# One head-blocked attention layer with a sign-weight branch: paired products and projections, split steps ahead of the joining maximum, a last output finished on VectorE

## What is computed

```python
xn = layernorm(x)
q = relu(xn @ Wq.T + bq); k = relu(keys @ Wk.T + bk); v = relu(values @ Wv.T + bv)
score = einsum('bhsd,bhtd->bhst', qh, kh) / sqrt(16.)
a = einsum('bhst,bhtd->bhsd', softmax(score), vh)
a = transpose(a, (0, 1, 3, 2)).reshape(q.shape)      # head-wise transposed
y = clip(xn @ sign(weights).T * scale + bias, -100, 100)
out = x + (a + xn) + y
```

## Time and profile before

| | |
|---|---|
| median of 3 runs | 2849.71 us (2847.73 to 2850.22) |
| the profiled execution | 2850.59 us, its span 2848.8 us |
| PE matmuls busy | 2770.7 us, 97% |
| ACT busy | 2450.2 us, 86% |
| DVE busy | 2337.4 us, 82% |
| POOL busy | 938.4 us, 33% |
| granted PE clock, mean | 0.983 |

### The profile page before, as it was taken

The page is one execution under the profiler, slowest core; times in us unless marked ns, Lnnn a source line. Parts: engine busy times, 40 slices in busy tenths (PEclk is TensorE's granted clock), DMA queues, the critical chain, the costliest instruction groups (busy, mean ns, idle before and its releaser), DMA issues.

```text
span 2848.8 us, 61155 instructions
## 1 busy us (share of the span) xinstructions
PE 2770.7 (97%) x17860; PEld 1149.8 (40%) x17860; DVE 2337.4 (82%) x4578; ACT 2450.2 (86%) x2949; POOL 938.4 (33%) x845
## 2 busy tenths in 40 slices
PE   8899999999999999999999999999999999999996
PEld 4434444443444434444443444434444443444331
DVE  6788888888888888888888888888888888888940
ACT  4688888888888888888888888888888888888996
POOL 4304334242343314333242343314333242343001
PEclk8699999999999999999999999999999999999998
DMA  7111121121221121121121221121121121211111
GB/s 142 60 40 55 65 70 36 56 70 55 65 70 52 40 70 55 65 66 33 62 69 55 65 66 49 47 70 55 65 64 35 62 68 56 65 62 37 48 55 38
DMA packets 78637, 167.74 MB, mean 59 GB/s; under 512 B 28548, under 2 KB 32647, under 8 KB 76327
## 3 DMA queue, kind: packets, MB, share of 16 engines
q1 hardware_dynamic: 78374, 164.19, 19.2%
HBM read 36.71 MB, written 17.83 MB: 19 GB/s over the span
## 4 chain that ended last, share of the span: by engine, by line
PE 79%; issue 10%; DVE 7%; ACT 2%; POOL 1%; DVEq 0%; DMA 0%; POOLq 0%; ACTq 0%
PE value_ps L611 30%; PE ring L633 28%; PE score_ps L597 13%; DVE mx L959 5%; ACT probs L806 2%; PE score_ps L677 1%; PE score_ps L662 1%; PE score_ps L679 1%; PE score_ps L666 1%; PE score_ps L664 1%; PE ring L720 1%; POOL fin L1097 1%; PE score_ps L715 0%; DVE excess L934 0%; PE ring L700 0%
## 5 line engine op out<-in xcount | busy, mean ns | idle before, releaser
L806 ACT ACTIVATE probs<-score_ps 128x1024 f32<-128x1024 f32 x2048 | 1992.3, 1024 | 236.1 <-PE score_ps L597 229.9
L959 DVE TENSOR_REDUCE mx<-ring 128x1 f32<-128x512 f32 x2952 | 1900.1, 684 | 248.8 <-PE ring L633 224.5
L633 PE MATMUL ring<-kstack,qstack 48*128 48x512 f32 x3444 | 1168.4, 467 | 16.7 <-DVE mx L959 3.1
L611 PE MATMUL value_ps<-probs,vones 128*32 128x512 f32 x8192 | 1092.3, 605 | 1.1 <-ACT taken L813 0.4
L633 PEld LDWEIGHTS ring<-kstack,qstack 48*128 48x128 f32 x3444 | 490.1, 184 | 1071.0 <-DVE mx L959 1034.3
L597 PE MATMUL score_ps<-qstack,kstack 51*128 51x512 f32 x4096 | 814.1, 416 | 13.8 <-ACT probs L806 4.5
L934 DVE CUSTOM_DVE_ANT_0 excess<-ring,excess 128x512 f32<-128x512 f32 x512 | 353.1, 690 | 136.7 <-PE ring L633 119.1
L1097 POOL TENSOR_TENSOR dense<-dense,affine 128x512 f32<-128x512 f32 x128 | 164.4, 1284 | 866.7 <-ACT dense L856 865.2
L597 PEld LDWEIGHTS score_ps<-qstack,kstack 51*128 51x128 f32 x4096 | 393.6, 186 | 132.1 <-ACT probs L806 70.5
L822 ACT ACTIVATE excess<-ring 128x512 f32<-128x512 f32 x492 | 294.0, 597 | 1.4 <-PE ring L633 1.2
L611 PEld LDWEIGHTS value_ps<-probs,vones 128*32 128x32 f32 x8192 | 161.5, 108 | 320.7 <-issue 289.1
(11 more groups left out here) (93 smaller groups left out, 1417.2 us busy)
## 6 DMA issues: line engine op xcount, KB each, us to landing
qstack<-parts SPq DMA_DIRECT2D x768, 64.0 KB, 2.5
fin<-taken SPq DMA_DIRECT2D x256, 128.0 KB, 2.9
xin<-x SPq DMA_DIRECT2D x16, 1024.0 KB, 5.1
base_cur<-base_new SPq DMA_DIRECT2D x16, 1024.0 KB, 5.3
fin<-recip SPq DMA_DIRECT2D x32, 512.0 KB
out<-fin SPq DMA_DIRECT2D x32, 512.0 KB, 2.6
qstack<-proj SPq DMA_DIRECT2D x256, 12.0 KB
kstack<-base_cur SPq DMA_DIRECT2D x16, 128.0 KB, 6.0
```

What stands on the lines that cost most here:

```text
L611: mm = pe.matmul(value_ps[h4 * 32:(h4 + 1) * 32, :], vones[:, 2 * tp + c, hh * HALF + side * PAIRS + 2 * g + j, :, :], probs[:, q % 2 * GR ...
L633: pe.matmul(ps[:, :], qstack[nh][rows, pair, st * P:(st + 1) * P], keys, start=True, stop=True).then_inc(s_mm, 1)
L806: nc.scalar.activation(probs[:, q % 2 * GROUP + u % GROUP, :], score_ps[src][:, :], ACT.Exp, scale=EXP_SCALE).then_inc(s_probs, 1)
L959: nc.vector.tensor_reduce(most, src[:, :], AX.X, ALU.max).then_inc(s_mx, 1)
```

## The change

It does four things. (1) Two dense products, or two projections, go into one score tile, one in each bank; ACT takes both with one instruction of 1024 columns. Half 0 has jobs in duos 2, 8 (dense pairs) and 11 (projection pair), half 1 in duos 1, 3 (turns) and 9 (projection pair). (2) Split steps 0 and 1 stand ahead of the join of duo 25, steps 2 to 4 ahead of the join of duo 27; ROWS_DUO is 27; all eight aggregates stand ahead of the join of duo 23. (3) POOL's `base` works in pairs. (4) The last half's output is finished on DVE in two halves of the columns (`finish_end`), without packing, DRAM and POOL, and SP writes each half when it is ready. The start part keeps its single jobs.

```diff
-        JOBS = [[("dense", k, None) for k in range(2 * NA)] + [("project", a, 1) for a in range(NA)],
-                [("turn", a, None) for a in range(NA)] + [("project", a, 0) for a in range(NA)]]
-        JOB_DUOS = [[2, 4, 6, 8, 11, 13], [1, 3, 7, 9]]
+        JOBS = [[("dense", (2 * a, 2 * a + 1), None) for a in range(NA)] + [("project", (0, 1), 1)],
+                [("turn", (a,), None) for a in range(NA)] + [("project", (0, 1), 0)]]
+        JOB_DUOS = [[2, 8, 11], [1, 3, 9]]
         LEAD = 32
-        ROWS_DUO = 26
+        ROWS_DUO = 27
         RECIP_UNIT = 14
+        JOINS = 6
+        SPLIT_STEPS = {TILES + JOINS: (0, 1), TILES + 8 + JOINS: (2, 3, 4)}
         AGGREGATE_DUO = 23
...
@@ SP, half_step @@
+                if last and not (now or att):
+
+                    result = out[NB - 1].rearrange("(f p j) c -> f p (j c)", f=2, p=P)[1]
+                    for a in range(NA):
+                        cols = slice(a * BANK, (a + 1) * BANK)
+                        sp.wait_ge(s_end, 3 * a + 3)
+                        sp.dma_start(result[:, cols], fin[:, 1, cols]).then_inc(s_out, 16)
+                    return
...
@@ PE, do_job @@
+                    pe.wait_ge(s_xs, nb * NA + last + 1)
+                    ps = tile(b, to, s_qr, 4, oc * 2 + last + 1, hh)
                     cols = slice(oc * P, (oc + 1) * P)
+                    for n, k in enumerate(ks):
+                        dst = ps[:, n * BANK:(n + 1) * BANK]
...
+                    mm.then_inc(s_q, len(ks))
...
+                    for n, k in enumerate(ks):
+                        for j in range(2):
+                            dst = ps[:, (2 * n + j) * H:(2 * n + j + 1) * H]
...
@@ ACT, take_job @@
-                    nc.scalar.activation(proj[:, k, :], score_ps[src][:, 0:BANK], ACT.Relu,
-                                         bias=bq_sb[:, oc:oc + 1]).then_inc(s_qr, 1)
+                    act.wait_ge(s_q, nb * 4 + oc * 2 + last + 1)
+                    nc.scalar.activation(proj[:, first:last + 1, :],
+                                         score_ps[src][:, 0:len(ks) * BANK].rearrange("p (n s) -> p n s", s=BANK),
+                                         ACT.Relu, bias=bq_sb[:, oc:oc + 1]).then_inc(s_qr, len(ks))
...
+                    wait(act, s_badd, nb * 4 + last - 1)
+                    act.wait_ge(s_f, nb * 4 + last + 1)
                     ps = value_ps if src is None else score_ps[src]
+                    nc.scalar.activation(dense[:, first % 2:last % 2 + 1, :],
+                                         ps[:, 0:len(ks) * BANK].rearrange("p (n s) -> p n s", s=BANK),
+                                         ACT.Copy).then_inc(s_dense, len(ks))
...
@@ DVE @@
+            def finish_end(a):
+
+                cols = slice(a * BANK, (a + 1) * BANK)
+                dve.wait_ge(s_gather[a], NB * 4 * 32)
+                nc.vector.reciprocal(fin[:, 1, cols], fin[:, 1, cols]).then_inc(s_end, 1)
+                dve.wait_ge(s_end, 3 * a + 1)
+                nc.vector.tensor_tensor(fin[:, 0, cols], fin[:, 0, cols], fin[:, 1, cols], ALU.mult).then_inc(s_end, 1)
+                dve.wait_ge(s_bcopy, NB * 16)
+                dve.wait_ge(s_end, 3 * a + 2)
+                nc.vector.tensor_tensor(fin[:, 1, cols].rearrange("p (q j) -> p q j", j=J),
+                                        base_cur[:, 1, cols].rearrange("p (q j) -> p q j", j=J),
+                                        fin[:, 0, cols].rearrange("p (j q) -> p q j", j=J), ALU.add).then_inc(s_end, 1)
...
                         for n in itertools.chain(*maxima_of(d)):
                             if prep and d in STATS_DUOS and n % 8 in STATS_AHEAD:
                                 statistics(b, *ROW_TILES[2 * STATS_DUOS.index(d) + STATS_AHEAD.index(n % 8)])
+                            if prep and d == AGGREGATE_DUO and n % 8 == JOINS - 1:
+                                dve.wait_ge(s_stats, (b + 2) * 8)
+                            for k in SPLIT_STEPS.get(n, ()):
+                                split_maxima(b, hh, k, b * 2 * REDS + made(hh, TILES - 1))
+                            if prep and d == AGGREGATE_DUO and n % 8 == JOINS:
+                                for a, j in ROW_TILES:
+                                    aggregate(a, j)
                             reduce_bank(b, hh, n, at)
-                            if n >= TILES and not is_difference(n) and reductions(n - TILES) <= 5:
-                                split_maxima(b, hh, reductions(n - TILES) - 1,
-                                             b * 2 * REDS + made(hh, TILES - 1))
-                    if last and d == RECIP_UNIT // 2:
+                    if last and (now or att) and d == RECIP_UNIT // 2:
                         reciprocals(*last)
-                    if prep and AGGREGATE_DUO <= d < AGGREGATE_DUO + 4:
-                        for a, j in ROW_TILES[2 * (d - AGGREGATE_DUO):2 * (d - AGGREGATE_DUO) + 2]:
-                            aggregate(a, j)
...
@@ POOL, base @@
-                scaled(0)
-                shifted(0)
-                for k in range(1, 4):
+                for k in range(0, 4, 2):
                     scaled(k)
-                    clipped(k - 1)
                     shifted(k)
-                    if k == 3:
-                        pool.wait_ge(s_aff, whole * 2 + 8)
-                    summed(k - 1)
-                clipped(3)
-                summed(3)
+                    scaled(k + 1)
+                    clipped(k)
+                    shifted(k + 1)
+                    pool.wait_ge(s_aff, whole * 2 + 2 * k + 4)
+                    summed(k)
+                    clipped(k + 1)
+                    summed(k + 1)
```

## The result

The changed kernel takes 2873.38 us (median of 4 runs, 2869.72 to 2875.63) against 2849.89 us (4 runs, 2847.73 to 2850.22) on the same chip: 1.0084 times as long, interval 1.0073 to 1.0096, or 23.5 us more. Forecast were 2876 us and a range of 2850 to 2888. So the sign and the size came out.

What follows compares the result with a forecast made beforehand. TensorE (PE) was taken to bound the kernel, nearly full. Terms of +22.3+6.9+7.2+1.4-11.7 = +26.1 us on the profiled 2850.6 gave 2876.7, 2876 us as the median; range 2850 to 2888.

Steps and rivals of the forecast that it cites:

- The turn: Row maxima's turn behind banks 6 and 7 of duo 27, waiting for split step 4: +0.72 us each, 31 times, +22.3 us.
- joins 27 to 29 about 6.0 us apart: Sign that the forecast is right: this spacing of DVE's joining maxima around the turn, in every half.
- the wait for mcols: Sign that the forecast is right: the turn's weight load on PE waits near 1 us for mcols.
- Rival B: PE's wait on DVE in the next octet takes up the turn's slip: -22.3 us, 2854; chance 0.10.
- Steps 0 and 1: First two split steps, in DVE's 0.36 us hole ahead of the join of duo 25: cost nothing.
- the free lateness: In the plain octet, a join may be late by about 0.13 us for nothing.
- Dense pairs: Two dense products with one wide ACT copy that delays the relu and bank 5: +0.23 us a pair, +6.9 us.
- Rival A: The wider copies hold nobody, as relu and exponential find enough slack: 2856; chance 0.15.
- Projection pairs: Wider copy delays the exponential, which holds the second scores' tile: +0.24 us a pair, 30 pairs, +7.2 us.
- Aggregates: All eight ahead of the join of duo 23, 0.64 us against 0.49 free: +0.1 us in 14 batches, +1.4 us.
- The end: Last half finished on DVE, with a 512-element reciprocal of 3.4 us: span ends at 2837.1, -11.7 us.
- Row transfers and GpSimd's base: Rows land with 1.3 us in hand; the second base pair ends later, but its transfers are wanted late: cost 0.

Runs made afterwards that it cites:

- run 5: Kernel before with the turn alone moved (ROWS_DUO = 27), split steps where they were: 2857.96 us, ratio 1.0032.
- Run 6: Changed kernel with ScalarE's copy of a dense pair cut to 512 of 1024 columns, second product left out of the output: 2864.30 us.
- Run 2: Kernel before with the moved split steps, aggregates and turn alone: 2873.45 us, ratio 1.0081.
- Run 4: Changed kernel with the turn one duo later (ROWS_DUO = 28): 2879.65 us, ratio 1.0107.
- run 1: Kernel before with the new end alone: 2837.05 us against 2850.01, ratio 0.9957.
- run 3: Kernel before with the products and projections in pairs alone: 2860.15 us, ratio 1.0039.
- run 9: Kernel before with the new end, and half 1's reciprocal moved ahead of the reduction of bank 3 of duo 7: 2832.48 us.
- run 8: Kernel before with the new end, products and projections in pairs, dense pair behind banks 1 and 2, its copy behind the relu: 2856.76 us.

## Why the prediction was right, and where it wasn't

The measure is the octets before and after, per batch of 171.3 us.

- **The turn, forecast +0.72 a half.** Measured for the whole move is +0.82 in half 1 and +0.85 in half 0. In half 1 the octet of duo 27 is 0.20 longer than one without a turn and that of duo 29 0.73, 0.93 together in place of the forecast 1.10; less the 0.38 of before that is +0.55. In half 0 the two are 0.51 and 0.74 longer, because of the slower cast, and it is +0.85. That the average of the two is near the forecast is luck. "The turn loads at -0.45+0.75 = 0.30" was nearly right: counted from where the join would have been, it loads at 0.21. What was wrong is "Everything behind the turn on PE (scores, bank 0, weighing, bank 1) is 1.10 us late, and by the cycle above that is the octet's cost": the join of duo 27 stands behind the same split steps and moves by 0.20 with them, and bank 0 loads 0.75 us behind that join because of the ring, here and in run 5, though the turn of run 5 is 0.27 us earlier and waits for no split step. So of the signs, "joins 27 to 29 about 6.0 us apart" did not come (5.64), and the wait for mcols is 0.58 us in half 1 and 0.87 in half 0, not near 1. I had read who waits for the turn, and not which bank the tile behind it takes. Rival B (no dearer than today) is excluded by the octets of 5.64.
- **Steps 0 and 1, forecast nothing: wrong.** They cost 0.28 us in half 1. "0.28 and 0.1 against 0.36 and 0.13" took the pitch of the second from a place in which other work follows. In the lines above step 0 to step 1 is 0.39 us and step 1 to the join 0.35, 0.74 for both; less the hole of 0.36 and the free lateness of 0.13 that leaves 0.25. So the 0.13 of free lateness fits to 0.03 us.
- **Dense pairs, forecast +0.23 each: size right, wait half right.** Measured 7.39 + 4.91 - 12.10 = +0.20. Rival A (octets of 7.0) falls. Run 6 shows both halves of the step, the 0.20 saved and the 0.43 lost to the copy (0.37). It doesn't separate bank 5 from the scores' tile, which I had put into the bounds alone and which waits longer (0.71).
- **Projection pairs, forecast +0.24 each: too high.** The pair's octet is 7.67 us (7.72 forecast) and the one behind it 5.06 (5.15), together 12.73 against 12.62 of the two single ones: +0.11 in half 0, and +0.07 in half 1, so 2.7 us in 15 batches and not 7.2. The wait for the exponential is there and longer than forecast (0.31 against 0.25), but only 0.15 us of it reaches the octet behind (5.06 against a plain 4.91). The part that failed is that the wait's "+0.25 us on PE" goes into the time in full; what takes up the rest was not tried. The third octet, 5.04, is the same in both kernels.
- **Aggregates, forecast +0.1 in half 0, and "GpSimd's root starts earlier, and nobody waits for it".** Run 2 against run 5, which differ in the split steps and aggregates alone: +0.54 us in half 0 and +0.47 in half 1, so +0.07 for the aggregates. But the sum hides three parts: octet 23 gets 0.10 longer, octet 25 gains 0.11 where in half 1 it loses 0.27, and octet 27 loses 0.55 where in half 1 it loses 0.20. Some 0.3 us of this last loss is the cast of step 3: in each kernel with the moved aggregates (the changed one, runs 2, 4 and 6) 14 of 32 of these casts take 0.46 to 0.49 us, and these 14 are the ones beside GpSimd's `xn`, which starts earlier behind the earlier aggregates; the other 18 have no GpSimd work beside them and take 0.2, as all do in the kernels without the move. That is 4 us of the change's loss which the forecast did not see. Why the cast takes longer is not shown, and no run parts the aggregates from the split steps.
- **The end, forecast -11.7 us: right** (-11.6 in the trace and in run 1). The reciprocal of 512 elements is 3.35 us (forecast 3.4). The Trainium skill's repeat count of 8 (VectorE: DVE Perf Modes, "First, the fixed hardware budget"), from which I had worked out an estimate of 4.3 us, is not borne out: the two lengths of the trace, 543 ns for 64 elements and 3354 ns for 512, give 6.3 ns an element and 0.14 us beside. The last addition is 1.03 and not 0.69 us; its operands are strided.
- **Row transfers and GpSimd's base, forecast nothing: right.** The list of waits has one wait for rows, 1.4 us in the start part, and none in a batch; no engine waits longer for GpSimd in a batch (the slower cast above is no wait). Run 4 shows the price when the rows come 2 us later.
- **The sum.** Turn and split steps forecast 22.3 and aggregates 1.4, measured 1.65 x 15 = 25; pairs forecast 14.1, measured 0.53 x 15 = 8; end -11.7 and -11.6. The first is 1 too low and the second 6 too high, so the forecast terms come to 21 and not to 26.1. That the medians differ by 23.5 and the profiled executions by 24.2 is luck in part: the first batch of the loop has 4 us from the fall of the clock, and the start part gives 2 back.

The rule of the Trainium skill that the forecast cites (VectorE: DVE Perf Modes, "The TRN2 errata"), that fixed costs are paid per instruction and large tiles spread them, holds for ScalarE's copy (1.03 us against 2 x 0.60) and not for the kernel: run 3 shows the loss.

## What to carry to other kernels

Before an operation is put into a rotating set of buffers, write down which buffer each of the next users takes with it and when that one comes free; the right gap was two tiles away from the wrong one, and worth 0.5 us of 0.74. Short dependent operations cost more when they stand together, so spread them among other work rather than collect them in the widest hole. Work that starts earlier can also fall beside an instruction that then takes longer: look at the durations of unchanged instructions too, and not only at waits. And a merged copy on an engine with idle time is still dear when something short is queued behind it or a double-buffered tile hangs on it.

## What the runs showed of the hardware

**Small dependent VectorE operations.** Before, each split step has a reduction behind it that doesn't need it; the timeline of the kernel before:

```profile
1208.85 0.28 DVE L968 TENSOR_REDUCE mneg<-mx 128x64 f32<-128x128 f32 x1
1209.04 0.68 DVE L959 TENSOR_REDUCE mx<-ring 128x1 f32<-128x512 f32 x1
1209.64 0.19 DVE L973 CAST mcols<-mneg 128x64 bf16<-128x64 f32 x1
1209.74 0.69 DVE L959 TENSOR_REDUCE mx<-ring 128x1 f32<-128x512 f32 x1
```

The reduction begins 0.19 us after step 0 and 0.10 after step 1, before either has ended. With the dependent step right behind, step 0 keeps the engine for 0.39 us (1226.73 to 1227.12). All five steps take 0.71 us of DVE when spread (0.19, 0.10, 0.13, 0.10 and 0.19) and 1.55 us in two groups (1226.73 to 1227.47 and 1231.77 to 1232.58). Of the 0.84 us between them 0.45 lie between dependent steps. The other 0.39 lie between the last step of a group and the join, which doesn't need it (0.35 and 0.33 from start to start); the profile names nothing that holds the join there. The Trainium skill (VectorE: DVE Perf Modes, "The DRAIN you can't avoid") says of a chain of copies that a semaphore after each costs nothing and that the next operation does not start until the pipe is empty, but also that one which is not held starts earlier; its section "Rules for kernel authors" advises to minimize the count of operations and not the semaphores. This trace agrees with the earlier start (0.10 us behind a step of 0.19). It disagrees with the advice for operations of 0.2 us: at the same count, the order doubles the time.

**The clock after a short idle.** In the profiled execution of the changed kernel TensorE's granted clock falls to half (1.2 of 2.4 GHz) behind the entry of the loop. The columns are busy us of PE, PEld, DVE, ACT and POOL, then the granted clock, DMA share and GB/s:

```profile
194.00:198.00 4.00, 2.68 (x19) 0.90 (x15) 3.66 (x7) 2.59 (x4) 0.00 (x0) 1.00 0.16 63
198.00:202.00 4.00, 3.87 (x21) 2.01 (x22) 1.69 (x4) 2.85 (x4) 0.00 (x0) 0.72 0.22 78
202.00:206.00 4.00, 4.00 (x18) 1.53 (x17) 2.39 (x4) 2.33 (x4) 0.00 (x0) 0.50 0.17 66
206.00:210.00 4.00, 4.00 (x18) 1.82 (x16) 1.40 (x4) 1.72 (x2) 0.00 (x0) 0.50 0.29 66
```

PE had been idle for 1.38 us just ahead, with no releaser in the profile. The kernel before has the same idle time (1.34 us) at the same place and stays at 1.00. All 14 profiled executions are idle there for 1.15 to 1.40 us, and in 3 the clock falls: in the changed kernel and run 9 for about 10 us, in run 6 for about 3. In the changed kernel it costs 4.3 us (octets of 8.59 and 9.52 where run 3 has 6.42 and 7.39). So an idle time of 1.3 us may or may not cost a further 4 us. In the start part the full clock comes back only at 120 to 122 us (run 1, the changed kernel) or at about 126 (the kernel before), not at 105 as the section on the time before has it, and the octet there is 7.5 to 7.8 or 9.6 to 10.1 us. Kernels with and without each part of the change are in both groups. Part of the spread of the runs is this: the 8 runs of the kernel before beside runs 1 to 4 go from 2848.06 us at a mean granted clock of 0.985 over 2849.6 and 2849.7 (0.984), 2849.6 to 2850.5 (0.983) and 2851.8 (0.982) to 2853.77 at 0.981.

**A late ScalarE.** In run 3, in the straight part behind the loop, an exponential whose scores are long done starts 1.45 us late (2662.93), PE stands, and the clock is 0.58 in the 4 us behind it; that is the octet of 7.62 us. The changed kernel has a smaller one (6.13 us, +1.3) there. Runs 4, 6 and 8 have it too: all five kernels with pairs have it once, with PE idle for 1.1 to 1.35 us, and none of the nine with single jobs. So as far as these traces tell it comes with the pairs; with the octets beside it, it costs 0.9 us in the changed kernel, 2.4 in run 3 and 3.8 in run 6. What holds ScalarE the profile doesn't show, and it was not tried.
